# A LoRA up product in three reduced-precision products, with half of the gate moved to GpSimd

## What is computed

```python
# x: (4, 256, 512); W_base (512, 512); W_gate (8, 512); A (8, 16, 512); B (8, 512, 16)
x = x + layernorm(attention(layernorm(x), wq, wk, wv, wo))
u = layernorm(x)
result = einsum('bnd,od->bno', u, W_base) + b_base
probs = softmax(einsum('bnd,ed->bne', u, W_gate))
top_p, top_i = top_k(probs, 2)
top_p = top_p / sum(top_p)
route_w = sum(one_hot(top_i, 8) * top_p[..., None], axis=-2)     # 8 weights, two of them not 0
h = einsum('bnd,erd->bner', u, A)                                # down product
delta = einsum('bner,eor->bno', h * route_w[..., None], B)       # up product
x = x + layernorm(result + delta)
```

## Time and profile before

| | |
|---|---|
| median of 3 runs | 239.64 us (237.5 to 241.78) |
| the profiled execution | 241.21 us, of which the span from the first to the last instruction is 239.4 us |
| mean granted PE clock | 0.986 |
| busy | PE 205.5 us, DVE 165.3, ACT 111.9, POOL 127.5 |
| instructions | PE 1304, DVE 342, ACT 197, POOL 126 |

### The profile page before, as it was taken

The page is one execution under the profiler, slowest core; times in us unless marked ns, Lnnn a source line. Parts: engine busy times, 40 slices in busy tenths (PEclk is TensorE's granted clock), DMA queues, the critical chain, the costliest instruction groups (busy, mean ns, idle before and its releaser), DMA issues.

```text
span 239.4 us, 3777 instructions
## 1 busy us (share of the span) xinstructions
PE 205.5 (86%) x1304; PEld 124.9 (52%) x1304; DVE 165.3 (69%) x342; ACT 111.9 (47%) x197; POOL 127.5 (53%) x126
## 2 busy tenths in 40 slices
PE   0599999997878699999999979889889979996870
PEld 0594834434544344445444314145768868985850
DVE  1882616778888766777777701457998898889675
ACT  2333531323023696787867775862512514433321
POOL 8200332653368596979736475883657365343332
PEclk9999999999999999999999999999999999998997
DMA  6998056986998127782932404044340010111022
GB/s 180 351 373 305 3 197 175 256 261 235 225 299 216 23 74 234 152 190 38 202 65 59 80 22 91 6 92 68 64 101 0 3 44 0 44 48 44 0 88 88
DMA packets 34065, 29.88 MB, mean 125 GB/s; under 512 B 3968, under 2 KB 29568, under 8 KB 34048
## 3 DMA queue, kind: packets, MB, share of 16 engines
q1 hardware_dynamic: 33536, 29.52, 46.1%
q10 hardware_dynamic: 512, 0.13, 0.3%
HBM read 17.19 MB, written 10.09 MB: 114 GB/s over the span
## 4 chain that ended last, share of the span: by engine, by line
PE 36%; DVE 26%; ACT 9%; issue 9%; DMA 7%; SPq 5%; POOL 4%; ACTq 2%; POOLq 1%; DVEq 0%
PE ps L1111 6%; DVE stats L761 5%; PE ps L1096 5%; PE ps L1070 4%; PE ps L1011 4%; ACT region_a L700 4%; PE ps L1001 3%; DVE nmax L938 3%; DVE gate L851 3%; PE ps L987 3%; DMA region_b<-q_scr 3%; PE ps L1159 3%; PE ps L1065 2%; SPq L337 2%; DMA x_sb<-x 2%
## 5 line engine op out<-in xcount | busy, mean ns | idle before, releaser
L938 DVE TENSOR_REDUCE nmax<-ps 128x4 f32<-128x1024 f32 x32 | 39.2, 1224 | 14.2 <-PE ps L1070 14.0
L524 POOL TENSOR_SCALAR_AFFINE_SELECT region_a<-region_a 128x1024 f32<-128x1024 f32 x32 | 35.3, 1108 | 19.1 <-ACT region_a L700 18.9
L700 ACT ACTIVATE region_a<-ps 128x1024 f32<-128x1024 f32 x32 | 32.8, 1024 | 0.9 <-PE ps L1096 0.8
L1096 PE MATMUL ps<-region_b,kst 98*128 98x512 bf16 x96 | 27.5, 382 | 3.5 <-ACT region_a L700 2.0
L1001 PE MATMUL ps<-region_a,region_c 128*128 128x512 f32 x64 | 29.0, 598 | 0.0
L571 ACT ACTIVATE std<-mv,eps_sb 128x1 f32<-128x1 f32 x32 | 9.3, 295 | 36.4 <-DVE mv L762 36.4
L935 DVE TENSOR_REDUCE nmax<-ps 128x4 f32<-128x512 f32 x32 | 21.9, 683 | 5.9 <-PE ps L1054 5.5
L1111 PE MATMUL ps<-region_a,v_aug 128*32 128x512 f32 x192 | 25.3, 603 | 0.6 <-POOL region_a L524 0.6
L697 ACT ACTIVATE region_a<-ps 128x512 f32<-128x512 f32 x32 | 19.2, 600 | 11.0 <-PE ps L1096 10.6
L516 POOL TENSOR_TENSOR x_sb<-x_sb,region_b 128x512 f32<-128x512 f32 x8 | 10.2, 1276 | 23.0 <-ACT region_b L636 23.0
L445 POOL TENSOR_TENSOR region_a<-region_a 128x512 f32<-128x512 f32 x4 | 6.5, 1629 | 28.4 <-DVE region_a L809 28.4
(11 more groups left out here) (103 smaller groups left out, 421.6 us busy)
## 6 DMA issues: line engine op xcount, KB each, us to landing
region_b<-q_scr SPq DMA_DIRECT2D x8, 768.0 KB, 6.3
q_scr<-region_c SPq DMA_DIRECT2D x8, 384.0 KB, 3.4
x_sb<-x SPq DMA_DIRECT2D x8, 256.0 KB, 6.1
q_scr<-region_c SPq DMA_DIRECT2D x8, 256.0 KB, 3.4
attn_t<-o_sb SPq DMA_DIRECT2D x32, 64.0 KB, 2.4
rden_bc<-r_scr SPq DMA_DIRECT2D x8, 256.0 KB, 3.2
out<-region_b SPq DMA_DIRECT2D x8, 256.0 KB, 2.0
kst<-k_scr SPq DMA_DIRECT2D x8, 192.0 KB, 3.9
```

The source lines that it names most:

```text
L524: pool.affine_select(out=blocks, in_=blocks, compare_op=ALU.is_ge, fill=0.0, base=0, pattern=[[0, 2], [0, REP], [1, P]], channel_multiplie ...
L700: nc.scalar.activation(probs[:, u % PRING, 1:3, :], ps[:, 4:6, :], ACT.Exp, scale=float(HEAD_DIM) ** -0.5).then_inc(exp_done, 1)
L938: nc.vector.tensor_reduce(nmax[:, gi % 2, 1, heads], ps[:, 1:3, :].rearrange("p a (r k) -> p r a k", r=REP), AX.XY, ALU.max, negate=True). ...
L1096: last = nc.tensor.matmul(ps[:, 3 + j, :], kst[0:TROWS, slot, k, kt * P:(kt + 1) * P], qst[0:TROWS, slot, k * REP:(k + 1) * REP, qt * P:(q ...
```

## The change

It touches three things. The up product of a tile becomes three terms of float32r parts, six products in place of two; the matrix `lora_b` is split in a ninth `SPLIT_WEIGHTS` step (n = 23), and the transposed row is split by ScalarE's copy out of PSUM, which now rounds to `hw_h`, and a new DVE subtraction `low_of_hw`. PE's up product now waits for that subtraction. GpSimd takes over 1 + e and the second one-hot. DVE's first one-hot is gone as an instruction: one `scalar_tensor_tensor` makes it and adds the second. The mask's float copy moves into a buffer that is free at that time.

```diff
-SPLIT_WEIGHTS = {15 + j: j for j in range(8)}
+SPLIT_WEIGHTS = {15 + j: j for j in range(9)}
...
+        lora_h = sb("lora_h", [P, DIM], F32R)
+        lora_l = over("lora_l", [P, DIM], "lora_b_sb", 0)
...
-        hw_t = region_b[:, 2304:2560].rearrange("p (a n) -> p a n", a=2)
+        hw_h = over("hw_h", [P, 2, P], "region_b", 2304)
+        hw_l = over("hw_l", [P, 2, P], "region_b", 7680)
...
                     pool.tensor_tensor(ga[:, 1:2], base_e[:, :], ga[:, 0:1], ALU.pow).then_inc(gexp_ready, 1)
+                    pool.wait_ge(gexp_ready, t3 + 1)
+                    pool.tensor_scalar(ga[:, 2:3], ga[:, 1:2], 1.0, None, ALU.add).then_inc(second_hot, 1)
+                    pool.wait_ge(index_ready, t3 + 1)
+                    pool.tensor_scalar(ga[:, 32:40], iota_sb[:, :], ga[:, 17:18], ga[:, 1:2],
+                                       ALU.is_equal, ALU.mult).then_inc(second_hot, 1)
...
-                    nc.scalar.copy(hw_t[:, t3 % 2, :], ps[:, 3, 0:P]).then_inc(hwt_ready, 1)
+                    nc.scalar.copy(hw_h[:, t3 % 2, :], ps[:, 3, 0:P]).then_inc(hwt_high, 1)
...
-                link(nc.vector.tensor_copy(ga[:, 16:18], gate_i[:, t % 2, 0:2]))
-                nc.vector.tensor_scalar(ga[:, 24:32], iota_sb[:, :], ga[:, 16:17], None, ALU.is_equal)\
-                    .then_inc(first_hot, 1)
+                nc.vector.tensor_copy(ga[:, 16:18], gate_i[:, t % 2, 0:2]).then_inc(index_ready, 1)
...
-                dve.wait_ge(gexp_ready, t + 1)
-                link(nc.vector.tensor_scalar(ga[:, 2:3], ga[:, 1:2], 1.0, None, ALU.add),
-                     nc.vector.tensor_scalar(ga[:, 32:40], iota_sb[:, :], ga[:, 17:18], ga[:, 1:2],
-                                             ALU.is_equal, ALU.mult))
-                dve.wait_ge(first_hot, t + 1)
+                dve.wait_ge(index_ready, t + 1)
+                dve.wait_ge(second_hot, 2 * t + 2)
                 link(nc.vector.reciprocal(ga[:, 3:4], ga[:, 2:3]),
-                     nc.vector.tensor_tensor(ga[:, 40:48], ga[:, 24:32], ga[:, 32:40], ALU.add))
+                     nc.vector.scalar_tensor_tensor(out=ga[:, 40:48], in0=iota_sb[:, :], scalar=ga[:, 16:17],
+                                                    in1=ga[:, 32:40], op0=ALU.is_equal, op1=ALU.add))
...
+            def low_of_hw(t):
+                dve.wait_ge(hwt_high, t + 1)
+                if t >= 2:
+                    dve.wait_ge(y_psum, t - 1)
+                nc.vector.tensor_tensor(hw_l[:, t % 2, :], ps[:, 3, 0:P], hw_h[:, t % 2, :].bitcast(F32), ALU.subtract)\
+                    .then_inc(hwt_low, 1)
...
                     ln_stats(3, t4, y_sb[:, t4 % 2, :])
+                if 0 <= t3 < TILES:
+                    low_of_hw(t3)
+                if 0 <= t4 < TILES:
                     if t4 < TILES - 1:
                         ln_scale(3, t4)
...
-                    pe.wait_ge(hwt_ready, t)
+                    pe.wait_ge(hwt_low, t)
...
             def up_projection(t):
-                pe.wait_ge(hwt_ready, t + 1)
-                nc.tensor.matmul(ps[:, 4 + 2 * (t % 2), 0:CATH], hw_t[:, t % 2, :], lora_b_sb[:, 0:CATH],
-                                 start=False, stop=True, skip_group_check=True)
-                nc.tensor.matmul(ps[:, 5 + 2 * (t % 2), 0:YB], hw_t[:, t % 2, :], lora_b_sb[:, CATH:DIM],
-                                 start=False, stop=True, skip_group_check=True).then_inc(y_psum, 1)
+                if t == 0:
+                    pe.wait_ge(weight_low, 9)
+                pe.wait_ge(hwt_low, t + 1)
+                terms = ((hw_h, lora_h), (hw_h, lora_l), (hw_l, lora_h))
+                for i, (part, w) in enumerate(terms):
+                    nc.tensor.matmul(ps[:, 4 + 2 * (t % 2), 0:CATH], part[:, t % 2, :], w[:, 0:CATH],
+                                     start=False, stop=(i == 2), skip_group_check=True)
+                    last = nc.tensor.matmul(ps[:, 5 + 2 * (t % 2), 0:YB], part[:, t % 2, :], w[:, CATH:DIM],
+                                            start=False, stop=(i == 2), skip_group_check=True)
+                last.then_inc(y_psum, 1)
```

More of the change, by code:

```diff
@@ L120, in build @@
         ident_bf = sb("ident_bf", [P, P], BF16)
-        mask_f = sb("mask_f", [P, P])
         mask_bf = sb("mask_bf", [P, REP, P], BF16)
@@ L161, in build @@
         qst = region_b[:, :].bitcast(BF16).rearrange("p (s h n) -> p s h n", s=RING, h=GROUP_HEADS)
+        mask_f = region_b[:, 8192:8320]
         xn_sb = region_b[:, 4096:8192].rearrange("p (t n) -> p t n", t=TILES)
@@ L250, in build @@
         top_ready = sem("top_ready")
-        first_hot = sem("first_hot")
+        index_ready = sem("index_ready")
+        second_hot = sem("second_hot")
         gexp_ready = sem("gexp_ready")
@@ L254, in build @@
         hwt_psum = sem("hwt_psum")
-        hwt_ready = sem("hwt_ready")
+        hwt_high = sem("hwt_high")
+        hwt_low = sem("hwt_low")
         y_psum = sem("y_psum")
@@ L271, in build @@
         quarters = [(w[:, j, :], h[:, j, :], l[:, j, :]) for w, h, l in ((wo_sb, wo_h, wo_l), (wcat_sb, wcat_h, wcat_l))
-                    for j in range(4)]
+                    for j in range(4)] + [(lora_b_sb[:, :], lora_h[:, :], lora_l[:, :])]
         def wait_o(engine, count):
```

## The result

The changed kernel takes 240.78 us (median of 9 runs, 240.41 to 242.37); the kernel before, in runs beside it, 238.91 (9 runs, 237.5 to 241.78). The ratio is 1.0085, 95% interval 1.0043 to 1.0127: slower by 0.9%, which is within 2% and yet clear of no change. Ratios here leave out, as slow runs, those over 1.5% above the fastest of their own kernel. The figure lies in the forecast range, the direction is wrong.

The account below looks back on a forecast made before the run. No engine was taken to bound the whole; PE runs without a hole in the pipeline's middle. Terms 0.5 - 3.1 + 1.1 = -1.5 us, set against the median 239.64, gave 238.1 us; range 236.0 to 242.2.

Parts of the forecast that it names:

- A: Three pipeline steps, from tile 1's transposes to tile 4's: 0.5 us lost (0 to 1.7).
- B: Two middle steps, from tile 4's transposes to tile 6's: PE's 0.12 us goes into waiting, 0 a step.
- C: Step behind the last projection, to tile 7's transposes: smaller holes, clock staying at 1.0, 3.1 us gained.
- D: Last tile, from tile 7's transposes to DVE's end: gate and low part later, 1.1 us lost.
- The baseline: Profiled execution of the kernel before, 241.21 us, would become 239.7; the sum was set against the runs' median, 239.64.
- The waits of PE for the low part: Tiles 0 to 2, ahead of the up product: about 0.5, 0.8 and 0.8 us, less 0.12 each.
- T + 7.8: Tiles 0 to 2: low part ready 7.8 us after the start of the step's four transposes (L1143).
- The up product: Six PE products per tile: 0.745 us (0.70 to 0.89) in place of 0.86, 0.12 less a tile.
- POOL's pair: GpSimd's two added gate instructions, 1 + e and the 8-element second selection: 0.2 and 0.27 us.
- the rival: GpSimd's two added instructions slow, 0.5 and 0.8 us: 3.3 us lost in tiles 0, 1, 2, 7; 245.0; chance 0.08.
- POOL ahead in the middle steps: Rival: POOL's sum starts before DVE's joined instruction; 0.2 us more in each of three steps; 241.7; chance 0.13.
- the low clock under the last up product: Rival: clock falls all the same, there or behind the last projection, taking back 1.38 us; 239.5; chance 0.22.

Follow-up runs that it names:

- Two kernels above: Changed kernel with unused PE products in the last tile, ratio 1.0062; changed kernel with tile 7's low part ahead of tile 6's last statistics, ratio 1.0023.
- output sum behind the gate: Changed kernel with GpSimd's output sum waiting for hw in the steps of tiles 2 and 7: 238.69 us, ratio 0.9981.
- the up product alone: Kernel before with only the three-term up product, its low part and the ninth weight split, gate as before: 241.14 us, ratio 1.0100.
- PE's late wait: Changed kernel with PE's wait for the low part moved to the third term only: 240.06 us, ratio 1.0039.
- the gate alone: Kernel before with only GpSimd's 1 + e and second selection and DVE's joined instruction, plain float32 up product: 241.24 us, ratio 1.0081.

## Why the prediction was wrong

Against the kernel before at full clock, the four stretches of the changed kernel give A +1.2 to +1.9, B +0.2, C -1.63, D +1.6 to +2.0, in all +1.4 to +2.5 (the medians: 240.78 - 238.91 = 1.87). The prediction had +0.5, 0, -3.1, +1.1, so -1.5. Of the 3.4 between that and +1.9, 1.4 is the baseline, and the rest is A, D and B.

*The baseline, the largest single error.* "I expect the clock to stay at 1.0: 1.06 and 0.32 back on the two terms": that 1.38 is a gain over the one profiled execution. Four of six executions never had the loss. The sum was then set against the median, 1.57 lower, and the text even gave both figures without asking why they differ. Without it, the same sum gives -0.1: no change. That the kernel became slower is in A and D.

*C, apart from that,* was right: 3.1 - 1.38 = 1.7 forecast, 1.63 measured, and by the steps named: the joined instruction ahead of POOL's sum (0.26 forecast, 0.27 measured in the middle, 0.28 in C), one hole of 0.67 left in place of two.

*A was mis-sized*, 0.5 for 1.2 to 1.9, at the end of its bounds (0 to 1.7). Two kernels above that differ from the changed one only in the last tile have an A of 28.1 and 28.3, so part of the 1.9 is the spread of executions. The waits of PE for the low part were in (0.20, 0.47, 0.48 measured, 0.5, 0.8, 0.8 forecast). The steps of A hold the gates of tiles 0, 1 and 2. They took 8.7 to 9.3, 8.6 to 8.7 and 9.6 before; they take 9.3 to 9.9, 8.8 and 10.1 now.

In tile 1's step more than half of the wait is made up, as forecast: of 0.47, 0.2 is left, the hole ahead of the transpose of `hw`, 0.19 in the profile before, having gone. The term that failed is in tile 2's step. The prediction names among its signs a joined instruction of about 1 us there, but puts no price on it: it counts the low part ready at T + 7.8, and it came at T + 9.2. POOL starts its sum right behind its two new instructions and ahead of the joined one, which takes 1.07 for that. The hole ahead of the transpose of `hw` grew from 0.52 to 1.31; in the kernel before it reads:

```profile
196.13 0.33 PE L1169 MATMUL ps<-ident_sb,region_b 128*128 128x128 f32 x1 [0.52 <-DVE region_b L867]
```

The output sum behind the gate takes 0.88 off this step and brings A to 27.4, inside the 26.9 to 27.5 of the kernel before. The 0.6 of tile 0's step was not isolated: the same hole is 0.5 to 1.1 there before and 0.8 to 1.5 after.

*B* was put at 0 and lost 0.2: tile 4's up product waits 0.22 for the low part. Tile 6's, for which the prediction had 0.4 in D, shows no such wait.

*The up product* was sized at 0.745 and took 0.86 where PE waits ahead of it, 0.76 where it does not. So splitting it gained PE nothing to 0.1 a tile, and left the wait.

*POOL's pair*: 0.2 and 0.27 forecast, 0.23 and 0.42 measured, far from the 1.0 at which the rival decides. *POOL ahead in the middle steps* did not occur in the changed kernel. Where PE's wait is late it did, and the steps grew no longer, so the 0.2 a step of that rival is not borne out there.

*D was mis-sized*, 1.1 for 1.6 to 2.0. The mechanism was the one named: 1.07 behind POOL's sum, then the low part behind the statistics. Missing were 0.2 of POOL's pair, and the low clock under the last up product (0.3 to 0.7), which had been a rival by itself: it occurred in both profiles of the changed kernel and in that of the up product alone, in none of six of the kernel before under its last up product.

*The rule on shared access* (SBUF — State Buffer, Who interferes with whom, of the Trainium skill), that the one that starts first holds the other up, held on both sides in the changed kernel: the joined instruction took 0.21 where it started 0.27 or more ahead of POOL's sum or alone, 1.07 where the sum had started 0.22 before it. At leads of 0.00 and 0.02 by the trace DVE was the one that stood still (1.30 and 1.33), so a lead of a few hundredths in a profile decides nothing.

## What to carry to other kernels

Before setting a sum against a profile, look at how that execution lies among the runs, and remove what only that execution has, a stretch of low clock first. An instruction that stands still behind another engine may lose nothing: if the engine that follows it would wait for the same queue anyway, taking the stall away can turn it into an idle time of the same length, as in tile 2's step. And where two engines contend for access, order them by one wait on the one with slack; here that was worth more than moving the work.

## What the runs showed that was not expected

The granted clock fell to 0.50 after idle stretches of PE that other executions of the same kernel pass at 1.0: the kernel before has holes of 1.24 and 0.78 us in step C in all six profiles, and fell in two. Under the last up product it fell in three of three profiles with 0.6 to 1.1 us of idle time ahead of the last transpose of `hw` and 1.47 behind it. With the first cut to 0.19 (output sum behind the gate), with the second cut to 0.68 (low part first), or with unused products in both, it did not fall before the product was over. Nor did it with 1.42 ahead of the transpose and then 0.35 and 0.34 (PE's late wait). In tile 2's step it fell behind a hole of 1.87 (the gate alone) and stayed at 1.0 behind one of 1.82 (PE's late wait). What decides between two such executions no run here shows.

Three float32r terms of 324 and 188 columns cost PE 0.76 to 0.86 us, the plain float32 product 0.86. Of the six, one of 188 columns costs 0.09 and one of 324 columns 0.17, more than the 0.148 of a long series of them.
